# Queries computed in channel rows, the key-token product split at the end of the step, and the vertical box sums done by three accumulating transfers

## The chip, the cores and the metric

The kernel runs on one core of a Trainium2 chip. Its time is the device time of one execution in microseconds (us); lower is better. Before the change it is 1625.53 us, the median of three runs (1621.58 to 1627.81).

## What is computed

Four residual layers are applied in turn to 32 images of 256 channels and 28 x 28 pixels in float32, each on a group-normalised copy of its input:

```python
x = x + _L0_conv_ref(_gn(x), ...)   # gate: sparsemax over 8 experts, then a mixed 1x1 convolution
x = x + _L1_conv_ref(_gn(x), ...)   # 3x3 depthwise, relu, prune, 1x1 convolution, relu, prune
x = x + _L2_conv_ref(_gn(x), ...)   # attention over the 784 pixels ("tokens")
x = x + _L3_conv_ref(_gn(x), 0)     # 3x3 box filter, every weight 1/9
```

The attention squares centred queries and keys and never forms a token-by-token matrix:

```python
q = q - jnp.mean(q, axis=2, keepdims=True); k = k - jnp.mean(k, axis=2, keepdims=True)
q2 = q * q; k2 = k * k
k2n = k2 / (k2s + EPS_DIV); q2n = q2 / (q2s + EPS_DIV)       # sums over the 256 channels
k2n = k2n / jnp.maximum(jnp.linalg.norm(k2n, axis=-2, keepdims=True), EPS_NORM)   # over the tokens
q2n = q2n / jnp.maximum(jnp.linalg.norm(q2n, axis=-1, keepdims=True), EPS_NORM)   # over the channels
kv = jnp.einsum('bnc,bnd->bcd', k2n, v)
out = (v + jnp.einsum('bnc,bcd->bnd', q2n, kv) / math.sqrt(N)) @ Wln + bln
```

## The kernel before

A channel row is a tile of 128 partitions (channels) by 784 columns (pixels); an image has two of them, j = 0 and 1. A token tile has 112 pixels on the partitions and 256 channels in the columns; an image has seven.

**The pipeline.** The program is a hand-written software pipeline. In step t each engine works on seven images at once, called Z, A, B, C_, D, E and F from the youngest to the oldest (Z is image t+1, F is image t-5). Z is loaded and its sums taken; A gets layer 0; B the depthwise convolution; C_ the 1x1 convolution of layer 1; D the queries and keys; E the attention weights and the layer's output; F the box filter and the store. There are 38 steps, t = -1 to 36; from t = 4 to t = 31 the attention stages D and E are both full and A is active too, and these 28 are called full steps below. On each engine the order of the work is the order in which its own `step` function calls the parts, and it never varies; engines wait for each other only through counting semaphores (`wait_ge`).

**TensorE's step**: `value_out(0)`, `key_norms`, `q_to_channels` (two of four pieces), `attention_weights`, `q_to_channels` (two), `value_out(1)`, `gate_logits(A)`, `attention_out` (two), `mix_experts(A)`, `queries_keys(D)`, `pointwise(C_)` and `x2_to_tokens(D)` in turn, `mixed_conv(A)`, `keys_x(D)`, `key_sums(D)`, `group_means`. The last feeds the group norms of all layers, so VectorE's `variances` and `scales_shifts` open the next step.

**Queries before.** `queries_keys` computes queries and keys together, per token tile: a bias matmul and six float32r matmuls of 512 columns. ScalarE squares both halves with running sums (`square_qk`), takes the norms with seven more squares (`q_norms`), and scales the seven tiles (`scale_q`). In the next step TensorE transposes the scaled queries into channel rows (`q_to_channels`, 14 transposes), ScalarE and VectorE copy them as a high and a low part (`q_high`, `q_low`), and `attention_out` reads them. The attention weights come from the product of the keys with the tokens (`keys_x`), which ScalarE and VectorE split into two parts at the start of the next step (`kx_high`, `kx_low`).

**The box filter before.** VectorE adds three columns and then three rows (`box_sums`, four instructions over both halves) and adds a ninth of that to x3 (`make_x4`); SyncE then stores the image.

**PSUM.** `conv_ps` has two banks per half and is used in turn by value and attention output, `pointwise` and `mixed_conv`; `tile_ps` has three banks for everything in tokens and for the attention weights.

Of the kernel before, what the change touches and what calls it, by code (L numbers as in the profile page):

```python
# [5 lines left out]
ALU = mybir.AluOpType  # L6
ACT = mybir.ActivationFunctionType
# [18 lines left out]
BOX_STEPS = 4  # L26
# [15 lines left out]
NORM_EPS = 1e-12  # L42

# [68 lines left out]
def build(nc, x, gate_wT, gate_b, expert_rows, mix_pattern, dw_w, channel_params, pw_wT, w_qk, b_qk, w_vT, w_ln, group_mean, ident, out):  # L112
    with ExitStack() as ctx:  # L113
# [31 lines left out]
        bqk_mean = sb("bqk_mean", [1, 2])  # L145
        b_out = sb("b_out", [P, J])
# [13 lines left out]
        q2 = sb("q2", [TOK, M, C])  # L160
        k2 = sb("k2", [TOK, M, C])
        k4 = sb("k4", [TOK, M, C])
# [4 lines left out]
        qT_parts = sb("qT_parts", [P, 2, J, HW], F32R)  # L167
# [18 lines left out]
        gn_r = sb("gn_r", [P, 4, J])  # L186
        gn_s = sb("gn_s", [P, 4, J])
# [15 lines left out]
        qk_sum = sb("qk_sum", [TOK, 2, M])  # L203
        qk_eps = sb("qk_eps", [TOK, 2, M])
        qk_rec = sb("qk_rec", [TOK, 2, M])
        k_rec2 = sb("k_rec2", [TOK, M])
        q_nsq = sb("q_nsq", [TOK, M])
        q_norm = sb("q_norm", [TOK, M])
        q_alpha = sb("q_alpha", [TOK, 3, M])
# [25 lines left out]
        stored = DmaCount([sem("stored_even"), sem("stored_odd")])  # L235

# [26 lines left out]
        qk_mm = sig("qk_mm", M)  # L263
        q2_ready = sig("q2_ready", M)
        k2_ready = sig("k2_ready", M)
        rec_step = sig("rec_step", 3)
        q4_ready = sig("q4_ready", M)
        q_root = sig("q_root")
        alpha_step = sig("alpha_step", 3)
        qa_ready = sig("qa_ready", M)  # L270
# [14 lines left out]
        qT_mm = sig("qT_mm", 4)  # L285
        qT_hi = sig("qT_hi", 4)
        qT_lo = sig("qT_lo", 4)
# [4 lines left out]
        box_step = sig("box_step", BOX_STEPS)  # L292
        x4_ready = sig("x4_ready", J)
# [11 lines left out]
        def box_operands(n):  # L305


            inner = x3pad[:, :, 1:1 + H, 1:1 + W]
            sums = row_sums[:, :, 1:1 + H, :]
            return [(sums, x3pad[:, :, 1:1 + H, 0:W], inner),  # L310
                    (sums, sums, x3pad[:, :, 1:1 + H, 2:2 + W]),
                    (inner, row_sums[:, :, 0:H, :], sums),
                    (inner, inner, row_sums[:, :, 2:2 + H, :])][n]
# [18 lines left out]

        QUADS = [(j, ms) for j in range(J) for ms in ([0, 1, 2, 3], [4, 5, 6])]

# [25 lines left out]
        def _(sp):  # L360
# [9 lines left out]
            def step(t):  # L370
                Z, F = t + 1, t - 5
# [5 lines left out]
                if F.active:  # L377
                    sp.wait_ge(x4_ready.sem, x4_ready.at(F))
                    sp.dma_start(out_dram[F.times(1)], x3[:, F.odd]).then_inc(stored.of(F), 16)

            run(sp, step)
            for last in (Image(None, IMAGES - 2), Image(None, IMAGES - 1)):
                sp.wait_ge(stored.of(last), stored.at(last))

# [913 lines left out]
```

## Time and profile before

| | |
|---|---|
| Three runs | 1621.58, 1625.53, 1627.81 us |
| Profiled execution, own time | 1624.92 us |
| Its span (first to last instruction) | 1623.1 us, mean granted TensorE clock 0.973 |
| TensorE (PE) busy | 1530.0 us, 94% |
| VectorE (DVE) busy | 1376.0 us, 85% |
| ScalarE (ACT) busy | 1362.3 us, 84% |
| GpSimd (POOL) busy | 189.1 us, 12% |
| DMA | 34 GB/s over the span |

Busy time is the share of the span in which an engine had an instruction under way. Matmuls overlap and their ends are modelled, so what a group of them costs is read from the start of the group to the start of the next one, not from its busy time.

### The profile page before, as it was taken

How to read it: one execution, taken by the hardware profiler on the slowest of the kernel's cores; microseconds unless marked ns; L12 is line 12 of the kernel's file. 1: busy time of each engine (PE TensorE's matmuls, PEld its weight loads, DVE VectorE, ACT ScalarE, POOL GpSimd, SP SyncE). 2: the span in 40 equal slices, each digit the busy share in tenths (PEclk: the TensorE clock that was granted, in tenths of full speed). 3: DMA queues.
4: the chain of work that ended last, by engine and by line, in shares of the span. 5: the costliest groups of instructions: out<-in, count | busy, mean ns of one | idle time of the engine just before them, and what ended most of it. 6: DMA issues, size and time to landing. Idle time of an engine off the chain costs nothing. (4 is left out here: it accounts for less than half of the span.)

```text
span 1623.1 us, 26428 instructions
## 1 busy us (share of the span) xinstructions
PE 1530.0 (94%) x8190; PEld 1149.4 (71%) x8190; DVE 1376.0 (85%) x2466; ACT 1362.3 (84%) x3496; POOL 189.1 (12%) x142
## 2 busy tenths in 40 slices
PE   4469999999999999999999999999999999999993
PEld 2247777777777777777777777777777777776773
DVE  5877689999888998988889998888999988888446
ACT  3368998988999888899998889999888899987862
POOL 1111011011110101111011111101101111010000
PEclk8689999999999999999999999999999999999996
DMA  4000011000111110011111001111100011000001
GB/s 148 20 20 21 21 40 41 31 29 22 40 40 40 40 40 20 20 40 40 40 40 40 20 20 40 40 40 40 40 27 28 24 40 40 21 21 21 21 20 40
DMA packets 21058, 55.58 MB, mean 34 GB/s; under 512 B 2321, under 2 KB 3345, under 8 KB 21010
## 3 DMA queue, kind: packets, MB, share of 16 engines
q1 hardware_dynamic: 20914, 54.98, 9.6%
q8 instruction: 25, 0.41, 0.1%
q14 instruction: 23, 0.19, 0.0%
q10 hardware_dynamic: 96, 0.00, 0.0%
HBM read 29.29 MB, written 25.69 MB: 34 GB/s over the span
## 5 line engine op out<-in xcount | busy, mean ns | idle before, releaser
L770 DVE SCALAR_TENSOR_TENSOR h<-xpad,dw_sb,h 128x784 f32<-128x784 f32 x512 | 495.9, 1031 | 0.0
L541 PE MATMUL tile_ps<-wqk,xn_parts 128*112 128x512 f32 x1344 | 363.8, 425 | 0.0
L541 PEld LDWEIGHTS tile_ps<-wqk,xn_parts 128*112 128x112 f32 x1344 | 235.3, 175 | 79.6
L583 PE MATMUL tile_ps<-k,xT 112*128 112x256 f32 x896 | 205.2, 388 | 7.7 <-ACT xT L1026 7.7
L583 PEld LDWEIGHTS tile_ps<-k,xT 112*128 112x128 f32 x896 | 174.3, 195 | 40.2 <-issue 8.4
L449 PE MATMUL conv_ps<-h,pw_masked 128*128 128x392 f32 x512 | 180.5, 496 | 5.5 <-issue 5.5
L960 ACT ACTIVATE junk<-x 128x784 bf16<-128x784 f32 x192 | 162.3, 848 | 23.6 <-DVE x L797 15.5
L571 PE MATMUL conv_ps<-x,mixed 128*128 128x392 f32 (+1 forms) x512 | 175.1, 494 | 2.2 <-ACT mixed L994 1.1
L1234 POOL TENSOR_SCALAR pw_masked<-pw_sb,hmask 128x256 f32<-128x256 f32 x64 | 119.1, 1869 | 433.9 <-DVE hmask L778 425.5
L1221 POOL TENSOR_SCALAR xpad<-x,gn_r,gn_s 128x784 f32<-128x784 f32 x64 | 64.4, 1013 | 894.2 <-DVE gn_s L701 894.2
L449 PE MATMUL conv_ps<-xn_parts,w_out 128*128 128x392 f32 x768 | 152.7, 347 | 0.0
L449 PE MATMUL conv_ps<-qT_parts,attn_parts 128*128 128x392 f32 x768 | 144.4, 343 | 0.3
L571 PEld LDWEIGHTS conv_ps<-x,mixed 128*128 128x128 f32 x512 | 94.7, 190 | 68.4 <-issue 4.7
L449 PEld LDWEIGHTS conv_ps<-h,pw_masked 128*128 128x128 f32 x512 | 95.5, 192 | 64.6 <-issue 8.6
L1101 ACT ACTIVATE q<-tile_ps 112x256 f32<-112x256 f32 x224 | 86.4, 386 | 62.7 <-PE tile_ps L541 62.6
L449 PEld LDWEIGHTS conv_ps<-qT_parts,attn_parts 128*128 128x128 f32 x768 | 134.9, 188 | 1.5 <-issue 1.5
L449 PEld LDWEIGHTS conv_ps<-xn_parts,w_out 128*128 128x128 f32 x768 | 133.3, 188 | 0.0
L1007 ACT ACTIVATE junk<-x 128x784 bf16<-128x784 f32 x128 | 109.4, 855 | 1.8 <-issue 1.8
L1110 ACT ACTIVATE junk<-q,qk_rec 112x256 bf16<-112x256 f32 x224 | 110.3, 498 | 0.0
L1026 ACT ACTIVATE xT<-tile_ps,qk_rec 112x256 f32<-112x256 f32 x224 | 88.0, 478 | 14.2 <-DVE qk_rec L863 9.8
L1120 ACT ACTIVATE q<-q,q_alpha 112x256 f32<-112x256 f32 x224 | 92.6, 494 | 0.0
L538 PE MATMUL tile_ps<-bqk,ones 128*112 128x512 bf16 x224 | 86.3, 385 | 0.0
(138 smaller groups left out, 2646.9 us busy)
## 6 DMA issues: line engine op xcount, KB each, us to landing
x<-x SPq DMA_DIRECT2D x32, 784.0 KB, 4.3
out<-x SPq DMA_DIRECT2D x32, 784.0 KB, 3.4
expert_sb<-expert_rows SPq DMA_DIRECT2D x8, 256.0 KB, 5.2
x<-w_qk SPq DMA_DIRECT2D x1, 512.0 KB
x<-w_vT SPq DMA_DIRECT2D x1, 256.0 KB
x<-w_ln SPq DMA_DIRECT2D x1, 256.0 KB
pw_sb<-pw_wT SPq DMA_DIRECT2D x1, 256.0 KB
gmean<-group_mean SPq DMA_DIRECT2D x1, 64.0 KB, 3.8
```

Source lines behind the costliest of these rows:

```text
L449: mm = nc.tensor.matmul(conv_ps[:, 2 * j + a, 0:HALF], wt[:, half(j)], act[:, a * HALF:(a + 1) * HALF], start=(first and i == 0), stop=(la ...
L541: mm = nc.tensor.matmul(bank, xn2_parts[:, u, i, m * TOK:(m + 1) * TOK], wqk[:, v, i, :], start=False, stop=(i == J - 1 and u == 1))
L571: mm = nc.tensor.matmul(conv_ps[:, 2 * j + a, 0:HALF + more], mixed[:, i * C + j * P:i * C + (j + 1) * P], x0[:, A.odd, i, a * HALF:(a + 1 ...
L583: mm = nc.tensor.matmul(tile_ps[:, KX_BANK, i * C:(i + 1) * C], xT[:, m, half(i)], k2[:, m, :], start=(m == 0), stop=(m == M - 1))
L770: ins = nc.vector.scalar_tensor_tensor(acc, view, scalar, acc, ALU.mult, ALU.add)
L960: nc.scalar.activation(junk[:, j * HW:(j + 1) * HW], source[:, j, :], ACT.Square, accum_out=gn_in[:, layer, 2 + j:3 + j]).then_inc(gn_sums ...
L1007: nc.scalar.activation(junk[:, j * HW:(j + 1) * HW], x0[:, Z.odd, j, 0:HW], func, accum_out=gn_in[:, 0, first + j:first + j + 1]).then_inc ...
L1026: nc.scalar.activation(xT[:, m, :], tile_ps[0:TOK, XT_BANK[m // 2], m % 2 * C:(m % 2 + 1) * C], ACT.Identity, scale=qk_rec[:, 1, m:m + 1]) ...
L1101: nc.scalar.activation(q2[:, m, :], bank[:, 0:C], ACT.Square, accum_out=qk_sum[:, 0, m:m + 1]).then_inc(q2_ready.sem, 1)
L1110: nc.scalar.activation(junk[0:TOK, m * C:(m + 1) * C], q2[:, m, :], ACT.Square, scale=qk_rec[:, 0, m:m + 1], accum_out=q_nsq[:, m:m + 1]). ...
L1120: nc.scalar.activation(q2[:, m, :], q2[:, m, :], ACT.Identity, scale=q_alpha[:, 2, m:m + 1]).then_inc(qa_ready.sem, 1)
L1234: nc.gpsimd.tensor_scalar(pw_masked[:, j, :], pw_sb[:, j, :], hmask[:, j:j + 1], 0.0, ALU.mult, ALU.add).then_inc(pw_masked_ready.sem, 1)
```

## The change

Queries leave the token tiles. `keys` computes the keys alone (256 columns per token tile); `queries` computes the centred queries directly as channel rows in `conv_ps` (24 matmuls of 392 columns), and ScalarE squares them with the bias (`square_q`) into `q2`, now [128, 2, 784]. The sum over channels that the query norm needs runs over partitions now, so TensorE makes it: ScalarE squares again (`fourth_powers_q`), `query_sums` adds the channels by matmuls against ones (strip s of the partitions holds quarter s of the tokens), ScalarE takes the root, VectorE the reciprocal of a [128, 196] tile, and `query_scales` spreads it over all partitions by four matmuls. VectorE multiplies (`scale_q`), and the high and low parts are made from `q2` in SBUF. `kx_high` and `kx_low` move from the start of step t+1 to the end of step t.

The box filter's scale of 1/9 is folded into the normalisation of x3 (`box_scale`), x3 itself is stored as soon as it is made, VectorE makes only the sums of three columns (`box_row_sums`), and three transfers from GpSimd's queue add the rows above, at and below each row to the stored image in HBM (`add_rows`).

```diff
             def value_out(B, D, E, F, j):
-                wait_free((B, x1_ready, j + 1), (D, y_ready, j + 1), (F, x3_ready, j + 1))
+                wait_free((B, x1_ready, j + 1), (D, y_ready, j + 1), (E, q2_ready, j + 1))
-            def queries_keys(D):
+            def keys(D):
                 pe.wait_ge(xn2_lo.sem, xn2_lo.at(D))
...
-                for m in range(M):
-                    wait_free(*before[m])
-                    bank = tile_ps[0:TOK, QK_BANK[m], :]
-                    nc.tensor.matmul(bank, ones16[:], bqk16[:], start=True, stop=False)
...
+                for b in range(4):
+                    wait_free(*before[b])
+                    for s, m in enumerate(PAIRS[b]):
+                        dst = tile_ps[0:TOK, K_BANK[b], s * C:(s + 1) * C]
+                        nc.tensor.matmul(dst, ones16[:], bqk16[:, C:2 * C], start=True, stop=False)
...
+            def queries(D):
+                for j in range(J):
+                    wait_free((D - 1, x3_ready, j + 1), (D + 2, x1_ready, j + 1))
+                    conv_tile(j, by_parts(wqk[:, :, :, 0:C], xn2_parts)).then_inc(q_mm.sem, 1)
+            def query_sums(D):
+                pe.wait_ge(q4_ready.sem, q4_ready.at(D))
+                pe.wait_ge(xT_ready.sem, xT_ready.at(D, 4))
+                for j in range(J):
+                    for s in range(STRIPS):
+                        mm = nc.tensor.matmul(tile_ps[s * SUB:(s + 1) * SUB, Q4_BANK, 0:QUARTER], ones[:, 0:SUB],
+                                              q4[:, j, s * QUARTER:(s + 1) * QUARTER], start=(j == 0), stop=(j == J - 1),
+                                              skip_group_check=True)
+                mm.then_inc(q4_sum.sem, 1)
+            def query_scales(D):
+                pe.wait_ge(alpha_step.sem, alpha_step.at(D))
+                pe.wait_ge(xT_ready.sem, xT_ready.at(D, 6))
+                for a in range(2):
+                    for s in range(2):
+                        row = (2 * a + s) * SUB
+                        mm = nc.tensor.matmul(tile_ps[:, ALPHA_BANK[a], s * QUARTER:(s + 1) * QUARTER],
+                                              idn[:, row:row + 1].to_broadcast([P, P]), q_alpha[:, 1, :], start=True,
+                                              stop=True)
+                    mm.then_inc(alpha_mm.sem, 1)
...
+            def box_row_sums(F):
+                dve.wait_ge(x3pad_ready.sem, x3pad_ready.at(F))
+                dve.wait_ge(setup_pool, SETUP_POOL)
+                if (F - 1).active:
+                    for rows in rows_added:
+                        dve.wait_ge(rows.of(F - 1), rows.at(F - 1))
+                nc.vector.tensor_tensor(*row_operands(0), ALU.add).then_inc(row_step.sem, 1)
+                dve.wait_ge(row_step.sem, row_step.at(F, 1))
+                nc.vector.tensor_tensor(*row_operands(1), ALU.add).then_inc(row_step.sem, 1)
...
+            def scale_q(D):
+                for a in range(2):
+                    dve.wait_ge(alpha_mm.sem, alpha_mm.at(D, a + 1))
+                    tokens = q2[:, :, a * HALF:(a + 1) * HALF]
+                    nc.vector.tensor_tensor(tokens, tokens, tile_ps[:, ALPHA_BANK[a], 0:HALF].unsqueeze(1).to_broadcast([P, J, HALF]),
+                                            ALU.mult).then_inc(qa_ready.sem, 1)
...
+            def add_rows(F):
+                pool.wait_ge(row_step.sem, row_step.at(F))
+                pool.wait_ge(stored.of(F), stored.at(F))
+                for n in range(BOX_ROWS):
+                    if n:
+                        pool.wait_ge(rows_added[n - 1].of(F), rows_added[n - 1].at(F))
+                    hold(pool, "pool")
+                    rows = row_sums[:, :, n:n + H, :].rearrange("p j h w -> p j (h w)")
+                    pool.dma_start(out_dram[F.times(1)], rows, accum_op=ALU.add).then_inc(rows_added[n].of(F), 16)
```

In the setup TensorE now waits for VectorE's centred bias row before two small matmuls that turn the query bias into a column.

TensorE, a full step, the stretch from the transposes of the queries to the tokens of x2, before (tile names are the program's; `L541` is a matmul of queries and keys, `L466` a transpose; the pair `L538`, `L541` stands seven times, once shown):

```order
L466 MATMUL tile_ps<-idn,q 128x112 x7
L449 MATMUL conv_ps<-xn_parts,w_out 128x392 x12
L440 MATMUL small_ps<-gate_in,ones 128x8 x2
L449 MATMUL conv_ps<-qT_parts,attn_parts 128x392 x24
L558 MATMUL small_ps<-expert_sb,mix_w 32x512 x8
L538 MATMUL tile_ps<-bqk,ones 112x512
L541 MATMUL tile_ps<-wqk,xn_parts 112x512 x6
```

The same stretch after the change, on to the stretch before `mixed_conv` (`L457` with `wqk` is `queries`, `L555` is `query_sums`):

```order
L457 MATMUL conv_ps<-xn_parts,w_out 128x392 x12
L448 MATMUL small_ps<-gate_in,ones 128x8 x2
L457 MATMUL conv_ps<-q_parts,attn_parts 128x392 x24
L585 MATMUL small_ps<-expert_sb,mix_w 32x512 x8
L536 MATMUL tile_ps<-bqk,ones 112x256
L539 MATMUL tile_ps<-wqk,xn_parts 112x256 x6
...
L457 MATMUL conv_ps<-xn_parts,wqk 128x392 x24
L471 MATMUL tile_ps<-idn,xn 112x128 x12
L457 MATMUL conv_ps<-h,pw_masked 128x392 x8
L555 MATMUL tile_ps<-fourth,ones 32x196 x8
L471 MATMUL tile_ps<-idn,xn 112x128 x2
```

The transposes are gone, the seven pairs are half as wide, the queries' 24 matmuls stand behind them, and `query_sums` stands between the 1x1 convolution and the last transposes.

VectorE, a full step, from the box filter to the group norm's sums, before:

```order
L819 TENSOR_TENSOR row_sums<-row_sums,x3pad 128x2x784
L819 TENSOR_TENSOR x3pad<-row_sums 128x2x28x28
L819 TENSOR_TENSOR x3pad<-x3pad,row_sums 128x2x28x28
L770 SCALAR_TENSOR_TENSOR h<-xpad,dw_sb,h 128x784 x7
L859 TENSOR_SCALAR qk_eps<-qk_sum 112x14
...
L870 TENSOR_SCALAR q_alpha<-q_norm 112x7
L872 RECIPROCAL q_alpha<-q_alpha 112x7
L874 SCALAR_TENSOR_TENSOR q_alpha<-q_alpha,qk_rec 112x7
L797 SCALAR_TENSOR_TENSOR x,gn_in<-conv_ps,x 128x784 x2
L770 SCALAR_TENSOR_TENSOR h<-xpad,dw_sb,h 128x784 x5
L687 COPY gn_avg<-small_ps 128x16
```

The same stretch after (`L803` is a tap of the depthwise convolution, `L907` is `scale_q`, `L912` is `kx_low`):

```order
L853 TENSOR_TENSOR row_sums<-row_sums,x3pad 128x2x784
L884 TENSOR_SCALAR k_eps<-k_sum 112x7
...
L803 SCALAR_TENSOR_TENSOR h<-xpad,dw_sb,h 128x784 x9
L895 TENSOR_SCALAR q_alpha<-q_norm 128x196
L900 RECIPROCAL q_alpha<-q_alpha 128x196
L817 TENSOR_SCALAR ymask<-y_over 128x2
L821 SCALAR_TENSOR_TENSOR x,gn_in<-x,ymask 128x784 x2
L830 SCALAR_TENSOR_TENSOR x,gn_in<-conv_ps,x 128x784 x2
L907 TENSOR_TENSOR q<-q,tile_ps 128x2x392 x2
L803 SCALAR_TENSOR_TENSOR h<-xpad,dw_sb,h 128x784 x6
L912 TENSOR_TENSOR kx_parts<-tile_ps,kx_parts 128x512
L713 COPY gn_avg<-small_ps 128x16
```

The key sums' reciprocals now stand ahead of nine taps, the query norm's reciprocal ahead of x2 and x1, and six taps, `scale_q` and `kx_low` stand between x1 and the group norm.

On GpSimd's queue the three accumulating transfers stand behind this step's mask of the 1x1 weights (`mask_weights`) and ahead of the next step's `normalise_x1`, which writes `xpad`; the second and the third each wait for the one before to have landed.

## Rows read from the trace of the kernel before

**Rows 1.** Window of 27 steps: length, busy us of PE, PEld, DVE, ACT, POOL; clock

```profile
138.64:1407.04 1268.40, 1268.31 (x6889) 956.88 (x6889) 1135.86 (x2020) 1142.16 (x2942) 155.09 (x108) 1.00 0.09 33
```

**Rows 2.** TensorE's timeline, one full step: start, length, operation, instructions

```profile
1408.89 0.91 PE L466 MATMUL tile_ps<-idn,q 112*128 112x112 f32 x7
1409.64 0.69 PE L505 MATMUL tile_ps<-bv_ln,k_rows 128*128 128x256 f32 x2
...
1412.02 0.83 PE L466 MATMUL tile_ps<-idn,q 112*128 112x112 f32 x7
1412.62 2.39 PE L449 MATMUL conv_ps<-xn_parts,w_out 128*128 128x392 f32 x12
...
1415.21 4.51 PE L449 MATMUL conv_ps<-qT_parts,attn_parts 128*128 128x392 f32 x24
1419.66 1.92 PE L558 MATMUL small_ps<-expert_sb,mix_w 128*32 128x512 f32 x16
1421.51 0.42 PE L538 MATMUL tile_ps<-bqk,ones 128*112 128x512 bf16 x1
...
1432.79 2.79 PE L449 MATMUL conv_ps<-h,pw_masked 128*128 128x392 f32 x8
1435.42 1.47 PE L474 MATMUL tile_ps<-idn,xn 128*112 128x128 f32 x12
...
1439.58 5.45 PE L571 MATMUL conv_ps<-x,mixed 128*128 128x392 f32 x16
1444.87 6.21 PE L583 MATMUL tile_ps<-k,xT 112*128 112x256 f32 x28
1451.00 0.85 PE L486 MATMUL tile_ps<-k,qk_rec 112*32 112x256 f32 x11
```

**Rows 3.** ScalarE's timeline in a full step, 1x1 convolution's results and a token copy

```profile
829.85 1.04 ACT L1089 ACTIVATE x<-conv_ps,bn_shift,bn_scale 128x784 f32<-128x784 f32 x1
831.00 0.95 ACT L1081 ACTIVATE over<-x,below 128x784 bf16<-128x784 f32 x1
...
831.95 0.46 ACT L1026 ACTIVATE xT<-tile_ps,qk_rec 112x256 f32<-112x256 f32 x1
```

**Rows 4.** VectorE's timeline in the same step, from x1 to the attention weights

```profile
836.66 1.04 DVE L797 SCALAR_TENSOR_TENSOR x<-conv_ps,x 128x784 f32<-128x784 f32 x1
...
838.58 4.82 DVE L770 SCALAR_TENSOR_TENSOR h<-xpad,dw_sb,h 128x784 f32<-128x784 f32 x5
843.32 0.17 DVE L687 COPY gn_avg<-small_ps 128x16 f32<-128x16 f32 x1
...
847.51 1.04 DVE L833 TENSOR_TENSOR qT_parts<-tile_ps,qT_parts 128x448 fp32r<-128x448 f32 x2
848.47 0.62 DVE L767 TENSOR_SCALAR h<-xpad,dw_sb 128x784 f32<-128x784 f32 x1
849.46 0.88 DVE L846 SCALAR_TENSOR_TENSOR attn_parts<-tile_ps,k_inv,attn_parts 128x256 fp32r<-128x256 f32 x2 [0.37 <-ACT attn_parts L1050]
```

**Rows 5.** Groups of instructions by form: count, busy us, mean ns, idle before

```profile
L853 DVE TENSOR_TENSOR xn_parts<-xn,xn_parts 128x784 fp32r<-128x784 f32 x64 | 59.3, 969 | 3.1 <-ACT xn_parts L1058 3.1
L1058 ACT CAST xn_parts<-xn 128x784 fp32r<-128x784 f32 x64 | 51.1, 845 | 11.2 <-PE conv_ps L449 11.2
...
L863 DVE RECIPROCAL qk_rec<-qk_eps 112x14 f32<-112x14 f32 x32 | 7.7, 242 | 1.1
...
L872 DVE RECIPROCAL q_alpha<-q_alpha 112x7 f32<-112x7 f32 x32 | 6.4, 201 | 1.1
```

**Rows 6.** The page's DMA queue and its issues: KB each, us to landing

```profile
q1 hardware_dynamic: 20914, 54.98, 9.6%
...
x<-x SPq DMA_DIRECT2D x32, 784.0 KB, 4.3
out<-x SPq DMA_DIRECT2D x32, 784.0 KB, 3.4
```

**Rows 7.** VectorE's timeline in step 35: first box sum behind the last x3

```profile
1597.65 1.79 DVE L819 TENSOR_TENSOR row_sums<-x3pad 128x1568 f32<-128x1568 f32 x1
```

More of the change, by code:

```diff
@@ L235, in build @@
         stored = DmaCount([sem("stored_even"), sem("stored_odd")])
+        rows_added = [DmaCount([sem(f"rows{n}_added_even"), sem(f"rows{n}_added_odd")]) for n in range(BOX_ROWS)]
         gn = sig("gn", GN_DONE)
@@ L383, in _ @@
                 sp.wait_ge(stored.of(last), stored.at(last))
+                for rows in rows_added:
+                    sp.wait_ge(rows.of(last), rows.at(last))
         @block.tensor
@@ L399, in setup @@
                                               start=(d == 0), stop=(d == J - 1))
+                pe.wait_ge(setup_dve, SETUP_CENTRED)
+                for j in range(J):
+                    nc.tensor.matmul(tile_ps[:, 1, J + j:J + j + 1], bqk_row[:, half(j)], ones[0:1, 0:1], start=True, stop=True)
                 for d in range(J):
@@ L605, in step @@
                 if D.active:
-                    queries_keys(D)
-                if C_.active:
-                    pointwise(C_, range(1))
-                if D.active:
+                    keys(D)
+                    queries(D)
                     x2_to_tokens(D, range(3))
                 if C_.active:
-                    pointwise(C_, range(1, 2))
+                    pointwise(C_, range(2))
                 if D.active:
+                    query_sums(D)
                     x2_to_tokens(D, range(3, 4))
@@ L619, in step @@
                 if D.active:
+                    query_scales(D)
                     keys_x(D)
@@ L886, in step @@
                     scales_shifts(A)
-                if E.active:
-                    kx_low(E)
+                if F.active:
+                    box_scale(A, F)
                 if A.active:
@@ L892, in step @@
                     key_norms(E)
-                    q_low(E, range(2))
+                    q_low(E)
                 if B.active:
@@ L897, in step @@
                     attention_weights_low(E)
-                    q_low(E, range(2, 4))
                 if A.active:
@@ L911, in step @@
                 if F.active:
-                    box_sums(F, range(BOX_STEPS))
-                if B.active:
-                    depthwise(B, slice(3, 10))
+                    box_row_sums(F)
                 if D.active:
@@ L917, in step @@
                 if B.active:
-                    depthwise(B, slice(10, 13))
-                if F.active:
-                    make_x4(F)
+                    depthwise(B, slice(3, 12))
+                if D.active:
+                    q_scales(D)
                 if C_.active:
                     make_x2(C_)
-                if D.active:
-                    q_scales(D)
                 if B.active and not D.active:
-                    depthwise(B, slice(13, None))
+                    depthwise(B, slice(12, None))
                 if A.active:
                     make_x1(A)
+                if D.active:
+                    scale_q(D)
                 if B.active and D.active:
-                    depthwise(B, slice(13, None))
+                    depthwise(B, slice(12, None))
+                if D.active:
+                    kx_low(D)
             run(dve, step)
@@ L1193, in step @@
                 if D.active:
-                    scale_q(D)
+                    q_high(D)
+                    kx_high(D)
             run(act, step)
```

257 lines of the change are left out of this document (122 added, 135 removed).

## Prediction

> **What bounds the kernel now.** I read the table of windows first: over the 27 steps from step 4 to step 31 TensorE is busy for 1268.31 of 1268.40 us at clock 1.00, VectorE for 1135.86 and ScalarE for 1142.16 [rows 1]. A full step takes 1268.40 / 27 = 46.98 us, TensorE has no gap in it, and the other two have some 4.9 and 4.7 us each. So what they are relieved of is worth nothing by itself; what TensorE is given or relieved of counts 28 times, and so does any wait that is put in its way. I then read TensorE's timeline from group start to group start [rows 2], to price its work, and the timelines of ScalarE and VectorE [rows 3, 4], to see when the new links of the chain are done. The last x3 and what comes behind it [rows 7] give the end.
>
> **TensorE's own work, per full step.** Removed: queries and keys together, 1432.79 - 1421.51 = 11.28 us; the transposes of the queries, 1409.64 - 1408.89 = 0.75 and 1412.62 - 1412.02 = 0.60, 1.35 together, their short waits in it [rows 2]. Added:
> - Keys: 49 matmuls of 256 columns. Two rows price a float32r matmul: 24 of 392 columns in 1419.66 - 1415.21 = 4.45 us, 0.185 each, which is 392 / 2.4 = 163 ns and 22 more; 49 of 512 (bias ones among them) in 11.28, 0.230 each, 213 ns and 17 more [rows 2]. With 20 more on 107 ns: 0.128 x 49 = 6.27 us. The lower end is the bare column rate, 5.24.
> - Queries: 24 matmuls of 392 columns as in `attention_out`, 4.45 us.
> - `query_sums`: 8 float32 matmuls, 196 columns, on four strips side by side. `mix_experts` is that with 512 columns: 1421.51 - 1419.66 = 1.85 us [rows 2]. By columns 0.71, half as it stands 0.93; I take 0.9.
> - `query_scales`: 4 float32 matmuls of 196 columns over the whole array. Four of 392 take 1435.42 - 1432.79 = 2.63 us [rows 2], so 1.32; with a change of bank 1.4.
>
> Sum: 6.27 + 4.45 + 0.9 + 1.4 = 13.02 against 12.63: 0.39 us more per step, so TensorE alone would make 47.37. The work moved off the two slower engines is paid by the one that is full.
>
> **The chain through the query norm.** This is new: within the step it starts, TensorE waits for ScalarE and VectorE after the queries. I count from the start of the keys, T = 0. TensorE: keys until 6.27, queries until 10.72, three banks of x2's transposes (1.3) until 12.0, 1x1 convolution until 17.3, `query_sums` 18.2, last transposes 18.4, `mixed_conv` (1444.87 - 1439.58 = 5.29 [rows 2]) 23.7.
> ScalarE is free of the key squares and of x0's sums at about 8.2 (seven squares, four sums, as now), and squares the second half of the queries when they are there, 10.8 to 11.75. Then six token copies at 0.36 (831.95 + 0.36 is where the next group starts): 13.9. Two squares of 784 columns at 0.75, a cast of that size being 0.845 with its overlap [rows 5]: 15.4. Twice (831.00 - 829.85) + (831.95 - 831.00) = 2.10 us for y [rows 3]: 19.6; the last copy and the root of [128, 196]: 20.3.
> VectorE has come there early: two row sums instead of four (two x 1.8 saved, and `make_x4`'s two), but the reciprocal of the key sums is put ahead of the nine taps and waits until 8.2; the taps end near 17.4 and it then idles until 20.3. This idle time is where the relief of VectorE goes. From 20.3:
> - `q_scales`: a reciprocal of 196 columns. Two rows show 201 ns for 7 and 242 ns for 14 [rows 5], 5.9 ns a column, so 242 + 182 x 5.9 = 1.3 us, and 0.33 for the maximum ahead of it: 1.63. The lower bound is one column per cycle as in 784 columns in 969 ns, about 0.36 + 0.33.
> - x2: 2.12 (x1's time and the mask's 0.2); x1: 838.58 - 836.66 = 1.92 [rows 4].
> - `scale_q`: two of 784 columns. The nearest rows are the 969 ns of a subtraction of that size [rows 5]; 1.85 for two.
> - six taps instead of five: 4.74 / 5 x 6 = 5.69 [rows 4].
> - from the group norm to the end of `q_low`'s first pair 848.47 - 843.32 = 5.15, in which `kx_low` already stands [rows 4]; `q_low` is now 1.85 instead of 0.95 (848.47 - 847.51), `box_scale` 0.2: 6.25.
> - one tap 0.55 and the attention weights' low part 0.88 [rows 4].
>
> 1.63 + 2.12 + 1.92 + 1.85 + 5.69 + 6.25 + 0.55 + 0.88 = 20.9, so the weights are ready at 41.2, 0.1 for the signal. Behind them TensorE has `attention_out`, 4.45, and `mix_experts`, 1.85, before the next keys: a step of 47.6 us. TensorE itself would have been there at 47.37 - 6.30 = 41.1, so it waits 0.2 to 0.3. `query_scales` doesn't hold anybody: the scales are there at 22.0, TensorE comes at 23.7, and VectorE takes its result at 26.1. The row transfers need no wait by VectorE in this part either. 47.6 - 46.98 = 0.62, times 28: **+17.4 us**.
> The Trainium skill, VectorE: DVE Perf Modes, in the walkthrough of the 8-slice pipeline, has the reciprocal as an iterative divide with a repeat count of 8. At that, an estimate from its clock of 0.96 GHz, 196 columns take 1.6 us, and the step 0.3 us more, 8 us in all. The two rows show 5.9 ns a column where the page gives 8.3; the rows decide here.
>
> **Edges.** Setup: TensorE waits for the centred bias row, which VectorE makes, ahead of matmuls that it now does earlier; I take 1.5 us, an estimate of mine of less than 0.1%. Steps 3, 32, 33 and 34 have the queries but not all of the rest: 0.6 each, 2.4. In step 35 the transposes' 1.35 and some 0.35 of waits go, and step 34's tail is 0.8 longer: -0.9.
>
> **The end, one accumulating transfer at a time.** Now 1623.1 - 1597.65 = 25.45 us lie behind the last x3 [rows 7]: the box sums and x4 of image 30, the norm, the same for image 31 and a store. After the change image 30's row sums (3.65) are followed by three transfers in series, D each; image 31's row sums must wait for all three, because `row_sums` is one buffer; then its own three. So 3.65 + 3D + 3.65 + 3D, the norm hidden under the first three. The trace shows no accumulating transfer. It reads as much of HBM as a load of x (784 KB, 4.3 us to landing) and writes as much as a store (3.4) [rows 6]. From below D = 3.4, a plain store; from above a whole load and then a whole store, 7.7. The queue's 9.6% of 1623.1 us for 64 such transfers and the weights is some 2.3 us of data each [rows 6]; the read of the destination makes the data twice as much but the landing is waited for once: D = 4.3 + 2.3 = 6.6. That gives 7.3 + 39.6 = 46.9, **+21.4 us**.
> The Trainium skill, DMA: Bandwidth & Descriptors, in the anatomy of one DMA on GpSimd's path, gives 2.0 us and the bytes at 436 GB/s for a plain transfer; an estimate from it is 3.8 us, and the sum would be 17 us less. It says nothing of the read that an accumulation needs.
> Within a full step the transfers are covered: GpSimd's next work is `xpad`, behind the group norm's scales; the norm starts 14.5 us ahead of T (1421.51 [rows 2] - 1407.04, the window's end [rows 1]), so again at 32.5, and with 1.9 for the scales `xpad` is due 34 us after T. The first transfer can start at 6. Two landings and an issue must fit between, so they cost nothing while D is under 13 us. If that cover went, `xpad` would be late, and with it the first tap.
>
> **Sum**, on the profiled execution's 1624.9 us, which is 0.6 below the median: 1624.9 + 17.4 + 1.5 + 2.4 - 0.9 + 21.4 = 1666.7, say **1667 us**, slower by 2.6%.
>
> **Rivals.**
> - R1, TensorE's own work leads (no wait for the attention weights): 0.39 x 28 = 10.9 instead of 17.4, 1660 us. For it: the margin in my chain is only 0.2 us. Chance 0.15.
> - R2, cheap transfers: D near 3.6 with the chain as forecast, 18 less, 1649 us. For it, a store's 3.4; against it, the second stream. 0.15.
> - R3, the transfers hold GpSimd: D over 14.4 us, so that three don't fit in a step of 47.6 less 4 for the sums and their start. At 18 us a step is some 58, 1930 us. Nothing in the rows is near it. 0.05.
> - R4, faster: narrow matmuls issue at the bare column rate. Then the keys are 1.03 us shorter, and as the chain starts behind them, the step is 46.6; with the reciprocal at one column per cycle 46.3 (TensorE's own 46.3): -0.65 x 28 = -18, and with D = 3.4 the end +2. 1611 us. It decides when a 256-column matmul costs under 0.115 us; against it, both measured widths carry 17 to 22 ns. 0.05.
> - R5, no change: a step stays at 47.0 because ScalarE's and VectorE's legs are a little shorter than I count, and the transfers cost a store each: 1624.9 + 3 + 2 = 1630. 0.10.
>
> The forecast itself has 0.50, with a range of its own of 1650 to 1690. A difference of 0.5%, 8 us, is about what a measurement of this kernel can tell from no change. Faster only in R4: 0.05. Within it: R5, 0.10. Slower: 0.85. The range reaches down to 1635 (D = 3.4 with TensorE's own work alone is 1641) and up to 1698 (D = 7.7 and one more us of wait per step is 1701); R3, R4, R5 lie outside.
>
> **What would show it.** Right: full steps of 47.4 to 47.9 us; VectorE idle for 2 to 3 us ahead of the query norm's reciprocal and ahead of the key sums'; TensorE waiting 0.2 to 0.5 us for the attention weights; 256-column matmuls 0.128 us apart; the reciprocal 1.3 us; six transfers in series at the end. Wrong: a step at or under 47.0, a chain whose longest wait is elsewhere (xT, mixed_conv, `row_sums`), or D outside 3.4 to 7.7.

## The result, and the profile after

The changed kernel takes 1646.36 us (median of 4 runs, 1646.04 to 1646.63), the kernel before 1626.18 (4 runs, 1621.58 to 1627.81): a ratio of 1.0129, 95% interval 1.0110 to 1.0147. It is 1.3% slower; the forecast was 1667, its range 1635 to 1698. The profiled execution took 1646.53 us, span 1644.9.

The total is nearer to the forecast than its parts are. The same stretch of 27 full steps as in [rows 1], after; columns as there:

```profile
145.78:1400.31 1254.53, 1254.53 (x7805) 1014.07 (x7804) 1074.74 (x1915) 993.88 (x2050) 250.17 (x186) 1.00 0.39 84
```

A full step is 1254.53 / 27 = 46.46 us instead of 46.98. I had forecast 47.6. TensorE's timeline in one of them, against [rows 2]: the first two rows are one of the seven key tiles, then the last of them, and what follows.

```profile
1366.90 0.32 PE L536 MATMUL tile_ps<-bqk,ones 128*112 128x256 bf16 x1
1366.97 0.96 PE L539 MATMUL tile_ps<-wqk,xn_parts 128*112 128x256 f32 x6
...
1371.88 0.95 PE L539 MATMUL tile_ps<-wqk,xn_parts 128*112 128x256 f32 x6
1372.66 4.46 PE L457 MATMUL conv_ps<-xn_parts,wqk 128*128 128x392 f32 x24
1376.96 1.47 PE L471 MATMUL tile_ps<-idn,xn 128*112 128x128 f32 x12
1378.27 5.43 PE L457 MATMUL conv_ps<-h,pw_masked 128*128 128x392 f32 x16
1383.63 0.87 PE L555 MATMUL tile_ps<-fourth,ones 128*32 128x196 f32 x16
1384.43 0.43 PE L471 MATMUL tile_ps<-idn,xn 128*112 128x128 f32 x2
1384.70 5.45 PE L598 MATMUL conv_ps<-x,mixed 128*128 128x392 f32 x16
1389.98 1.49 PE L567 MATMUL tile_ps<-q_alpha,idn 128*128 128x196 f32 x8
1391.31 6.21 PE L610 MATMUL tile_ps<-k,xT 112*128 112x256 f32 x28
```

From start to start, the keys take 1372.66 - 1366.90 = 5.76 us, the queries 4.30, `query_sums` 0.80, `query_scales` 1.33: 12.19 for the 12.63 that went. VectorE's timeline in a full step, for the chain through the query norm (group starts; the bracket is the idle time ahead of it):

```profile
817.35 0.17 DVE L884 TENSOR_SCALAR k_eps<-k_sum 112x7 f32<-112x7 f32 x1 [1.94 <-ACT k L1133]
...
829.03 0.27 DVE L895 TENSOR_SCALAR q_alpha<-q_norm 128x196 f32<-128x196 f32 x1 [2.56 <-ACT q_norm L1158]
829.33 1.38 DVE L900 RECIPROCAL q_alpha<-q_alpha 128x196 f32<-128x196 f32 x1
...
845.57 2.47 DVE L858 TENSOR_TENSOR q_parts<-q,q_parts 128x784 fp32r<-128x784 f32 x2
847.97 0.61 DVE L800 TENSOR_SCALAR h<-xpad,dw_sb 128x784 f32<-128x784 f32 x1
848.51 0.86 DVE L871 SCALAR_TENSOR_TENSOR attn_parts<-tile_ps,k_inv,attn_parts 128x256 fp32r<-128x256 f32 x2
```

The keys start at 809.36 here. That is T. The query norm is there at T + 19.7 (forecast 20.3), the weights' low part at 849.37, T + 40.0 (forecast 41.2), and TensorE starts `attention_out` at 849.49, 0.1 us later and without a gap that the profile shows. This view can't tell whether TensorE waited there a little or was only just done with its own work; experiments 6 and 7 can.

The end is where the time went. First VectorE behind the last x3, against [rows 7], then GpSimd, then the page's rows on the transfers, against [rows 6]:

```profile
1589.69 1.79 DVE L851 TENSOR_TENSOR row_sums<-x3pad 128x1568 f32<-128x1568 f32 x1
...
1616.37 1.79 DVE L851 TENSOR_TENSOR row_sums<-x3pad 128x1568 f32<-128x1568 f32 x1 [21.70 <-DMA out<-row_sums]
```

```profile
1593.91 1.20 POOL L1270 DMA_DIRECT2D out<-row_sums  x1 [26.15 <-DVE row_sums L853]
1601.60 1.19 POOL L1270 DMA_DIRECT2D out<-row_sums  x1 [6.49 <-DMA out<-row_sums]
1609.23 1.19 POOL L1270 DMA_DIRECT2D out<-row_sums  x1 [6.44 <-DMA out<-row_sums]
1620.60 1.22 POOL L1270 DMA_DIRECT2D out<-row_sums  x1 [10.18 <-DVE row_sums L853]
1628.45 1.21 POOL L1270 DMA_DIRECT2D out<-row_sums  x1 [6.63 <-DMA out<-row_sums]
1635.95 1.20 POOL L1270 DMA_DIRECT2D out<-row_sums  x1 [6.29 <-DMA out<-row_sums]
```

```profile
q0 software_dynamic: 26112, 77.08, 28.8%
...
out<-row_sums POOLq DMA_DIRECT2D x96, 784.0 KB, 7.1
x<-x SPq DMA_DIRECT2D x32, 784.0 KB, 5.5
out<-x SPq DMA_DIRECT2D x32, 784.0 KB, 3.5
```

One accumulating transfer lands after 7.1 us, and the next is issued 7.5 to 7.9 us after the one before. Behind the last x3 there are 1644.9 - 1589.69 = 55.2 us, instead of 25.45.

The whole difference, by stretches of the two profiled executions:

| stretch | before | after | difference | forecast |
|---|---|---|---|---|
| start to the group norm of step 4 | 138.64 | 145.78 | +7.1 | +2.1 |
| 27 full steps | 1268.40 | 1254.53 | -13.9 | +16.7 |
| from there to the last x3 | 190.61 | 189.38 | -1.2 | +1.5 |
| behind the last x3 | 25.45 | 55.2 | +29.8 | +21.4 |
| span | 1623.1 | 1644.9 | +21.8 | +41.8 |

In the first row, step 0 has 28.55 us instead of 24.91, and TensorE's timeline there shows its wait (the second row is the experts' matmuls, on which the mixed weights and then ScalarE's square root for the batch norm wait):

```profile
22.50 1.01 PE L407 MATMUL tile_ps<-ones,xn 1*128 1x1 f32 x4 [4.38 <-DVE xn L684]
...
25.44 2.81 PE L585 MATMUL small_ps<-expert_sb,mix_w 128*32 128x512 f32 x16
```

### The profile page after: what moved, and what is told of

It is laid out like the page before. It is cut to its first block, busy times and chain, and to the rows that moved or that the text cites. A ratio compares the mean times of both kernels' runs of the same rounds, so it can differ in the third digit from the quotient of the medians.

```text
span 1644.9 us, 27605 instructions
## 1 busy us (share of the span) xinstructions
PE 1517.3 (92%) x9282; PEld 1219.7 (74%) x9282; DVE 1296.9 (79%) x2339; ACT 1186.2 (72%) x2440; POOL 304.0 (18%) x238
## 3 DMA queue, kind: packets, MB, share of 16 engines
q0 software_dynamic: 26112, 77.08, 28.8%
## 4 chain that ended last, share of the span: by engine, by line
PE 90%; DVE 4%; DMA 2%; ACT 2%; issue 1%; POOLq 0%; ACTq 0%; DVEq 0%
PE conv_ps L457 35%; PE tile_ps L610 12%; PE tile_ps L539 10%; PE conv_ps L598 9%; PE small_ps L585 4%; PE tile_ps L484 4%; PE tile_ps L471 3%; PE tile_ps L567 3%; PE tile_ps L506 3%; DMA out<-row_sums 2%; PE tile_ps L503 2%; PE tile_ps L536 2%; PE tile_ps L555 2%; DVE h L803 1%; PE small_ps L448 1%
## 5 line engine op out<-in xcount | busy, mean ns | idle before, releaser
L803 DVE SCALAR_TENSOR_TENSOR h<-xpad,dw_sb,h 128x784 f32<-128x784 f32 x512 | 492.5, 1029 | 0.0
L1270 POOL DMA_DIRECT2D out<-row_sums x96 | 115.6, 1204 | 491.9 <-DMA out<-row_sums 411.2
L539 PE MATMUL tile_ps<-wqk,xn_parts 128*112 128x256 f32 x1344 | 187.4, 294 | 0.0
L457 PE MATMUL conv_ps<-h,pw_masked 128*128 128x392 f32 x512 | 176.3, 498 | 5.5 <-issue 5.5
L539 PEld LDWEIGHTS tile_ps<-wqk,xn_parts 128*112 128x112 f32 x1344 | 169.5, 175 | 0.1
L457 PE MATMUL conv_ps<-xn_parts,w_out 128*128 128x392 f32 x768 | 151.0, 345 | 0.0
L1256 POOL TENSOR_SCALAR xpad<-x,gn_rs 128x784 f32<-128x784 f32 x64 | 64.4, 1008 | 455.2 <-DVE gn_rs L727 455.2
L457 PEld LDWEIGHTS conv_ps<-h,pw_masked 128*128 128x128 f32 x512 | 96.1, 193 | 70.6 <-issue 9.4
L457 PE MATMUL conv_ps<-q_parts,attn_parts 128*128 128x392 f32 x768 | 145.3, 345 | 0.0
L457 PE MATMUL conv_ps<-xn_parts,wqk 128*128 128x392 f32 x768 | 142.7, 341 | 0.0
L457 PEld LDWEIGHTS conv_ps<-q_parts,attn_parts 128*128 128x128 f32 x768 | 135.9, 188 | 0.4 <-DVE attn_parts L871 0.3
L457 PEld LDWEIGHTS conv_ps<-xn_parts,wqk 128*128 128x128 f32 x768 | 135.7, 188 | 0.0
L457 PEld LDWEIGHTS conv_ps<-xn_parts,w_out 128*128 128x128 f32 x768 | 134.5, 188 | 0.0
L1142 ACT ACTIVATE q<-conv_ps,bq_col 128x784 f32<-128x784 f32 x64 | 58.6, 915 | 50.4 <-PE conv_ps L457 50.2
L1133 ACT ACTIVATE k<-tile_ps 112x256 f32<-112x256 f32 x224 | 84.2, 381 | 8.0 <-PE tile_ps L539 7.9
```

The lines of the kernel that those rows point to most:

```text
L457: mm = nc.tensor.matmul(conv_ps[:, 2 * j + a, 0:HALF], wt[:, half(j)], act[:, a * HALF:(a + 1) * HALF], start=(first and i == 0), stop=(la ...
L539: mm = nc.tensor.matmul(dst, xn2_parts[:, u, i, m * TOK:(m + 1) * TOK], wqk[:, v, i, C:2 * C], start=False, stop=(i == J - 1 and u == 1))
L803: ins = nc.vector.scalar_tensor_tensor(acc, view, scalar, acc, ALU.mult, ALU.add)
L1133: nc.scalar.activation(k2[:, m, :], tile_ps[0:TOK, K_BANK[m // 2], m % 2 * C:(m % 2 + 1) * C], ACT.Square, accum_out=k_sum[:, m:m + 1]).th ...
L1270: pool.dma_start(out_dram[F.times(1)], rows, accum_op=ALU.add).then_inc(rows_added[n].of(F), 16)
```

## The experiments

All ratios are against runs of the kernel before on the same chip. A step's time is that between two starts of VectorE's copy of the group means, over the same 27 full steps; the windows shown are those.

**1. The queries alone.** The changed kernel, with the box sums, x4 and the store as before:

```
-                    pool.dma_start(out_dram[F.times(1)], rows, accum_op=ALU.add)
+                nc.vector.tensor_tensor(*row_operands(2), ALU.add).then_inc(row_step.sem, 1)
+                nc.vector.tensor_tensor(*row_operands(3), ALU.add).then_inc(row_step.sem, 1)
...
+                    nc.vector.tensor_tensor(x4, x3pad[:, j, 1:1 + H, 1:1 + W], x4, ALU.add)
```

> The query part of the change without the box part: VectorE makes all four box sums and x4 again, and the store stands behind x4. Theory 1 (the two halves of the change need each other): VectorE gets two more sums of 128x1568 (1.8 us each) ahead of the key sums' reciprocal and two adds for x4 (0.97 us each) behind the query scales. The first 3.65 us are partly taken by its idle 1.94 and 2.56 us of the changed kernel; the 1.94 us of x4 lie in the chain from the query norm to the attention weights, which has no slack. So full steps of about 48.3 us instead of 46.46 (+53 us over 28), the end back to some 25 us behind the last x3 (-30): 1670 us. Theory 2 (TensorE's own work leads and VectorE has room): steps stay at 46.46, only the end goes back: 1617 us.

Measured: 1671.83 us, ratio 1.0281 (1.0266 to 1.0297). The window of 27 steps, and TensorE ahead of `attention_out` in one step:

```profile
146.25:1453.39 1307.14, 1271.21 (x7817) 1025.94 (x7815) 1212.53 (x2019) 993.08 (x2050) 153.73 (x108) 0.99 0.09 32
```

```profile
1121.29 4.55 PE L457 MATMUL conv_ps<-q_parts,attn_parts 128*128 128x392 f32 x24 [1.46 <-DVE attn_parts L878]
```

A step is 48.41 us, TensorE is idle for 35.9 us of the window, and the wait named is the one expected, that for the attention weights' low part. Theory 1 holds. Made alone, the query part of the change costs 2.8%.

**2. The transfers alone.** The kernel before with row sums, early store and three accumulating transfers; queries and keys untouched:

```
-                    box_sums(F, range(BOX_STEPS))
+                    box_row_sums(F)
-                if F.active:
-                    make_x4(F)
...
+                if F.active:
+                    add_rows(F)
```

> The box part of the change on the kernel of before: row sums on VectorE, three accumulating transfers, the store ahead; queries and keys as they were. Theory 1: full steps stay at 46.98 us, since TensorE has no gap and its work is the same, and the transfers are hidden in them; the end grows from 25.45 us to 7.3 + 6 x 7.7 = 53.5, so +28: about 1654 us. Theory 2: less work on VectorE and ScalarE makes full steps shorter too, as in the changed kernel (46.5 us, -14): 1640 us. Theory 3: the transfers disturb x's loads or GpSimd in the steps, which then are over 47.2 us: above 1660.

Measured: 1645.27 us, ratio 1.0121 (1.0105 to 1.0136).

```profile
139.35:1400.21 1260.86, 1260.86 (x6886) 956.08 (x6886) 1008.89 (x1942) 1136.50 (x2942) 252.43 (x186) 1.00 0.41 84
```

The end is as in theory 1: from the group norm of step 34 on it has 28.1 us more than before. But a step is 46.70, not 46.98, with the same matmuls: between the two theories. So the kernel before had 0.28 us of waiting in each step that its window, "busy for 1268.31 of 1268.40", doesn't show. TensorE's timeline has the place of most of it: the second row starts 0.74 us after the first, and the third 0.26 after the second.

```profile
1355.86 0.91 PE L469 MATMUL tile_ps<-idn,q 112*128 112x112 f32 x7
1356.60 0.61 PE L508 MATMUL tile_ps<-bv_ln,k_rows 128*128 128x256 f32 x2
1356.86 1.06 PE L511 MATMUL tile_ps<-w_out,kx_parts 128*128 128x256 f32 x6
```

Before, in the step at 1360, the same two distances are 0.86 and 0.35, 0.21 us more, and VectorE's low part of the key-token sums, for which these matmuls wait, ends just as they start:

```profile
1361.99 0.91 PE L466 MATMUL tile_ps<-idn,q 112*128 112x112 f32 x7
1362.85 0.70 PE L505 MATMUL tile_ps<-bv_ln,k_rows 128*128 128x256 f32 x2
1363.20 1.06 PE L508 MATMUL tile_ps<-w_out,kx_parts 128*128 128x256 f32 x6
```

One view of the kernel before does name this wait: not in TensorE's matmuls but in its weight loads. From 420 to 1360 us the list of waits has `PEld tile_ps L505 <- DVE kx_parts L879: 3.6, 20, 0.2`, which is 3.6 us in 20 steps; the same list of this experiment has no such line. The lists of the other two engines point to a loop through both of them as what leads. VectorE waits 1.6 us a step for ScalarE's query norm, and ScalarE 0.5 us a step for VectorE's reciprocal of the sums (`ACT xT L1026 <- DVE qk_rec L863: 9.4, 19, 0.6`), ahead of which the four box sums stand. With two of them gone the second wait is gone too.

**3. The last two images on VectorE.** The changed kernel, with the 30 other images' vertical sums by transfers:

```
+        def by_vector(F):
+            return F.pair is None and F.offset >= VECTOR_FROM      # VECTOR_FROM = IMAGES - 2
...
                     box_row_sums(F)
+                    if by_vector(F):
+                        box_columns(F)
...
-                if F.active:
+                if F.active and not by_vector(F):
                     add_rows(F)
```

> The changed kernel, but the last two images have their vertical sums and x4 on VectorE and a plain store; the 30 others use the transfers. Theory 1 (the end is the six transfers in series and nothing else): behind the last x3 at 1590 us there are again some 25 to 27 us, so a span of about 1616 and 1618 us, 0.5% faster than before. Theory 2 (what the end costs is something else, such as the drain of earlier transfers, which the store waits for): above 1630 us.

Measured: 1617.56 us, ratio 0.9948 (0.9934 to 0.9961). The last x3 is done at 1591.00 us, the span ends at 1617.0: 26.0 us. Theory 1 holds. Against the changed kernel 28.8 us are saved, more than the 20 us that the change loses: that is what the six transfers in series cost beyond the same work on VectorE.

**4. The bias matmuls later.** The changed kernel, with the two matmuls on the centred bias row behind the experts':

```
                     mix_experts(A)
+                if t.first:
+                    setup_bias()
```

> The changed kernel with the two matmuls on the centred bias row behind the experts' matmuls in step 0, so that TensorE doesn't wait 4.38 us for VectorE ahead of them. Theory 1 (step 0's extra 3.64 us come from that wait through the mixed weights and ScalarE's square root for the batch norm): step 0 back to about 25 us, in all 1642.8 us. Theory 2 (VectorE's own setup sets step 0): 1646 us as it was.

Measured: 1642.88 us, ratio 1.0100 (1.0085 to 1.0116). Step 0 has 25.10 us, and the order in TensorE's timeline is

```profile
19.18 1.92 PE L588 MATMUL small_ps<-expert_sb,mix_w 128*32 128x512 f32 x16
22.44 0.60 PE L413 MATMUL tile_ps<-ones,xn 1*128 1x1 f32 x4 [1.33 <-DVE xn L689]
```

Theory 1 holds. The prediction had 1.5 us for this wait; it was 3.5.

**5. Halved columns.** The kernel before, its 512-column matmuls as pairs of 256:

```
-                    nc.tensor.matmul(bank, ones16[:], bqk16[:], start=True, stop=False)
+                    for cols in (slice(0, C), slice(C, 2 * C)):
+                        nc.tensor.matmul(bank[:, cols], ones16[:], bqk16[:, cols], start=True, stop=False)
```

> The kernel of before, with every 512-column matmul of queries and keys as two of 256 columns, 98 instead of 49 per full step, and nothing else. It prices the narrow matmul in the old surroundings. Theory 1 (a narrow matmul carries about the same 17 to 22 ns as a wide one, as the prediction had it): 98 x 0.128 = 12.54 us instead of 11.28, a full step 1.26 us longer, 29 of them: about 1662 us. Theory 2 (what the changed kernel showed, 0.1176 us each, is the price of the width): 98 x 0.1176 = 11.52, +0.24 us a step, about 1633 us. Theory 3 (the changed kernel's pitch has to do with its surroundings): somewhere between.

Measured: 1627.07 us, ratio 1.0006 (0.9997 to 1.0016). The first and the last of the 14 groups, and what follows:

```profile
1375.01 0.32 PE L539 MATMUL tile_ps<-bqk,ones 128*112 128x256 bf16 x1
...
1385.66 0.96 PE L542 MATMUL tile_ps<-wqk,xn_parts 128*112 128x256 f32 x6
1386.45 1.81 PE L449 MATMUL conv_ps<-h,pw_masked 128*128 128x392 f32 x5
```

11.44 us for 98, 0.1167 each: the width's own price, in old surroundings too, and theory 1 is out. The time is 1.6 us above the kernel before, not the 7 of theory 2, for the 0.16 us that TensorE does more per step don't appear: 27 steps take 1268.67 us instead of 1268.40. They went into the wait of experiment 2, whose two distances are now some 0.84 and 0.35 us in one step and 0.75 and 0.28 in the next. In the kernel before, the loop through VectorE and ScalarE led by some 0.2 us, not TensorE.

**6. A second reciprocal.** The changed kernel, with the chain 1.3 us longer:

```
                 nc.vector.reciprocal(q_alpha[:, 1, :], q_alpha[:, 0, :]).then_inc(alpha_step.sem, 1)
+                nc.vector.reciprocal(q_again[:], q_alpha[:, 0, :])
```

> The changed kernel with the reciprocal of 196 columns of the query norm made twice on VectorE, the second time into a tile that nobody reads. It adds 1.3 to 1.4 us to VectorE behind the query norm. Theory 1 (TensorE's own work and the chain through the query norm end within 0.1 us of each other, so the chain has no slack): full steps of 46.46 + 1.2 = 47.7 us, in all about 1681 us. Theory 2 (TensorE leads with a margin of over a microsecond): 1646 us as it was.

Measured: 1684.15 us, ratio 1.0359 (1.0343 to 1.0375). 27 steps take 1290.07 us, 47.78 each, 1.32 more, the length of the reciprocal; TensorE waits ahead of `attention_out`:

```profile
1016.33 4.55 PE L458 MATMUL conv_ps<-q_parts,attn_parts 128*128 128x392 f32 x24 [1.12 <-DVE attn_parts L872]
```

So the chain has no slack.

**7. No reciprocal.** The opposite, a chain 1.1 us shorter; this kernel leaves out the division by the query norm:

```
-                nc.vector.reciprocal(q_alpha[:, 1, :], q_alpha[:, 0, :])
+                nc.vector.tensor_scalar(q_alpha[:, 1, :], q_alpha[:, 0, :], 1.0, None, ALU.mult)
```

> The changed kernel with the reciprocal of the query norm replaced by a multiplication by 1 (the division by the norm is left out), so that VectorE's chain is some 1.1 us shorter per step. Theory 1 (TensorE's own work leads, the chain is just behind): full steps stay at 46.46, 1646 us. Theory 2 (the chain leads and TensorE waits for it in small pieces): full steps shorter by up to a few tenths, 1638 to 1643 us.

Measured: 1640.95 us, ratio 1.0090 (1.0075 to 1.0106). By the total this looks like theory 2. By the steps it is theory 1:

```profile
145.23:1399.47 1254.24, 1254.24 (x7804) 1013.17 (x7804) 1049.47 (x1915) 989.67 (x2051) 250.19 (x186) 1.00 0.40 84
```

1254.24 / 27 = 46.45, as it was. Nearly all of the gain lies at the end, where less work covers the chain: steps 32 to 34 have 42.98, 41.29 and 41.11 us instead of 44.93, 42.43 and 43.19. In the changed kernel TensorE's own work leads in a full step, and the chain is right behind it (experiment 6).

**8. Transfers that don't accumulate**, and **9. transfers of half the channels**, both on the changed kernel; 8 leaves out the vertical sums and the residual, 9 the vertical sums of each image's second 128 channels:

```
-                    pool.dma_start(out_dram[F.times(1)], rows, accum_op=ALU.add)
+                    pool.dma_start(out_dram[F.times(1)], rows)                                      # 8
+                    pool.dma_start(out_dram[F.times(1)][:, 0], rows[:, 0], accum_op=ALU.add)        # 9
```

> The changed kernel with the three transfers of row sums not accumulating: the same bytes from the same tile by the same queue, each overwriting the image (the vertical sums and the residual are so left out). Theory 1 (the read of the destination is what an accumulating transfer costs beyond a store): from issue to issue some 4.8 us instead of 7.7, so 6 x 2.9 = 17 us less at the end, 1629 us, full steps unchanged. Theory 2 (the cost is that of GpSimd's queue and of the way there and back): 7.7 us as before, 1646 us.

> The changed kernel with the accumulating transfers carrying the first 128 channels only, 392 KB instead of 784 KB (the vertical sums of the other channels are left out). Known: 7.1 us to landing for the full accumulating transfer, 3.8 for the full plain one. Theory 1 (one fixed time, the rest by bytes): with 2.0 us fixed, 4.6 to landing, 5.1 from issue to issue, 15 us less at the end, 1631 us. Theory 2 (the way there and back is made twice, the read ahead of the write, so two fixed times): 5.6 to landing, 6.2 from issue to issue, 9 us less, 1637 us. Theory 3 (bytes don't matter): 1646 us.

Measured: 1627.62 us for 8, ratio 1.0013 (1.0004 to 1.0022), and 1635.05 for 9, ratio 1.0053 (1.0038 to 1.0068). Of the page of 8, and then of 9:

```profile
q0 software_dynamic: 13824, 77.08, 11.9%
...
out<-row_sums POOLq DMA_DIRECT2D x96, 784.0 KB, 3.8
```

```profile
out<-row_sums POOLq DMA_DIRECT2D x96, 392.0 KB, 4.8
```

A plain transfer of the same bytes lands after 3.8 us. The Trainium skill, DMA: Bandwidth & Descriptors, in the anatomy of one DMA on GpSimd's path, has 2.0 us and the bytes at 436 GB/s; an estimate from it is 3.8 us, and for a plain transfer the trace agrees. The accumulating one takes 7.1 us, with nearly twice the packets (26112 for 13824), and doesn't follow that formula. Between 392 and 784 KB it grows from 4.8 to 7.1: 2.3 us for 392 KB, so 4.6 us that go with the bytes and 2.5 that don't. That is nearer to theory 1 of run 9 (4.6) than to theory 2 (5.6), and so is the time from issue to issue at the end, 5.3 to 5.4 us for theory 1's 5.1 and theory 2's 6.2. The total is not: 1635.05 us lies nearer to theory 2's 1637 than to 1631. Some 2 us of that lie in the last wait of SyncE's queue, for TensorE's (3.9 us for 1.7 in the changed kernel), which neither theory had; why it is longer is open. So what the accumulation adds goes mostly with the bytes, as far as two sizes can show. The full steps of both stay at 46.46 us.

**10. The key-token sums split early, alone.** The kernel before, with the third part of the change only:

```
-                if E.active:
-                    kx_low(E)
                 if A.active:
                     gate_logits(A)
...
                     depthwise(B, slice(13, None))
+                if D.active:
+                    kx_low(D)
```

ScalarE's `kx_high` moved likewise.

> The kernel of before with one thing of the change alone: the two parts of the key-token sums are made at the end of the step in which the sums arise, on ScalarE and VectorE, and not at the start of the next, behind the group norm. Theory 1 (in the kernel before, TensorE waits some 0.2 to 0.3 us per full step for these parts, unseen inside the time of its matmuls, and the changed kernel owes half of its gain per step to that): full steps of 46.7 instead of 46.98 us, about 8 us less, 1618 us. Theory 2 (the wait is one for VectorE as a whole, and only the relief by the box sums takes it away): 1626 us as before.

Measured: 1639.83 us, ratio 1.0080 (1.0067 to 1.0094). Slower, which neither theory had. A step is 1280.73 / 27 = 47.43 us. VectorE now waits at the end of the step for ScalarE's part, ahead of the group norm:

```profile
852.87 0.69 DVE L879 TENSOR_TENSOR kx_parts<-tile_ps,kx_parts 128x512 fp32r<-128x512 f32 x1 [1.15 <-ACT kx_parts L1127]
```

ScalarE's part stands there behind its scaling of the seven query tiles. TensorE's wait for the key-token sums is gone from the list of waits, but VectorE's new one costs more, and TensorE now waits 0.5 us a step for ScalarE's copy `k_rows` and 0.3 for its `k_norm`, for which it didn't before. So theory 1's gain isn't there, and what the place of the split would be worth without these new waits, this run can't tell. That the relief by the box sums takes the 0.28 us away without the split, experiment 2 shows. Which of the operations taken from VectorE would be enough was not tried; the list of waits there points at the two ahead of the reciprocal of the sums.

**11. Both edges mended**: 3 and 4 together, a version that beats both kernels.

> The changed kernel with both edges mended: the last two images' vertical sums and x4 on VectorE with a plain store, and the two bias matmuls of the setup behind the experts' matmuls. If the two gains are independent they add: 1646.4 - 28.8 - 3.5 = 1614 us, 0.7% faster than before. If step 0's gain is taken back by a later wait: 1617.5 us.

Measured: 1614.11 us (5 runs, 1612.24 to 1615.09), ratio 0.9930 (0.9916 to 0.9943). The gains add up: 1646.4 - 28.8 - 3.5 = 1614.1.

## Why the prediction was right or wrong

- **Direction and range: right, the direction in part by luck.** The time lies 21 us below the forecast, in the range of 1635 to 1698 but outside the 1650 to 1690 of the forecast's own case. That case (the chain leads, 47.6 us a step) is not what happened: the full steps were to lose 16.7 us and gained 13.9, and only the ends made the kernel slower. By mechanism the rival R1 is nearest, since TensorE's own work leads, though with less of it than R1 had. By the number R2 (1649) is nearer, but its cheap transfers are not what was found.
- **"Keys: 49 matmuls ... 0.128 x 49 = 6.27 us": the step that failed.** They took 5.76, 0.1176 each. I had added a fixed 20 ns to the column time, as from the two widths shown. Measured: 256 columns 0.1167 to 0.1176 us, 392 columns 4.30 / 24 = 0.179, 512 columns 0.230. That is 0.46, 0.46 and 0.45 ns a column; what I read as a fixed cost goes mostly with the width. (The 24 of `attention_out` take 4.45 us before and 4.47 after, 0.186 each; why those of `queries` take less is open.) With it the queries (4.30 for 4.45), `query_sums` (0.80 for 0.9) and `query_scales` (1.33 for 1.4; no run shows the 0.08 us that I had added for a change of bank) were too dear, together by 0.83 us. R4 was built on this very price, with 0.115 us as the point where it decides; the runs came close to that, and I had given it 0.05.
- **"TensorE has no gap in it": a misreading, 0.28 us.** The base of the sum, 46.98, held a wait that hid inside the groups' times; experiments 2 and 5 show it. Steps then went 46.98, less 0.28 by the relief of experiment 2 (46.70), less 0.24 by TensorE's work (46.46). Of the latter the four terms give 0.44; some 0.2 us come back where groups of matmuls follow each other in a new order (the 1x1 convolution with x2's transposes takes 6.94 us without `query_sums`, for 6.80 in experiment 2). The full step was off by 47.6 - 46.46 = 1.14 us: 0.83 and 0.28, less these 0.20, and the 0.23 of waiting for the weights that didn't come.
- **The chain: right in mechanism, late by 1.2 us.** Weights at T + 40.0 for 41.2: 0.66 because keys and queries are shorter, and most of the rest because VectorE waits 0.27 us for the group norm's root instead of 0.78; that `q_low` takes 0.6 more is made up for by two other small terms (no wait ahead of `kx_low`, shorter gate products). Both idle times of VectorE, 1.94 and 2.56 us, are where they were forecast. That the chain has no slack is shown by experiment 6, and that a shorter chain gains nothing in a full step, by 7: TensorE leads, by next to nothing.
- **The reciprocal: right**, 1.30 us from start to start for 1.3. An estimate from the repeat count of 8 in the Trainium skill, VectorE: DVE Perf Modes, in the walkthrough of the 8-slice pipeline, was 1.6 us; the trace doesn't agree, at 6.6 to 7 ns a column. `q_low` was too cheap, 2.47 us for 1.85. GpSimd writes `xpad` at that time; whether that is the cause was not tried.
- **"D = 4.3 + 2.3 = 6.6": right in mechanism, the term too small.** It is 7.1 us to landing and 7.7 from issue to issue, which is the upper bound of 7.7. Six times 1.1 is most of the 8.4 us that the end was off. That the transfers are hidden in a full step is right: the steps of experiments 8 and 9, with shorter transfers, are the same.
- **Setup: 1.5 for 3.5 us.** I priced the wait and not what hangs on it: the experts' matmuls, then the mixed weights, then ScalarE's root, then VectorE. The other edges: step 3 is 1.6 us longer, forecast 0.6. Step 2's 1.8 may in part be the clock's and not the change's: the same 16 matmuls of the 1x1 convolution took 8.56 us in the profile of experiment 4 and 7.21 in that of experiment 11, with the same code up to there, at a granted clock of 0.64 and 0.76; in the changed kernel 7.88, at 0.70, and before 7.04, at 0.78.

So the expected loss came, for another reason: the steady part of the kernel gained 14 us, and the two ends, which the change touches by the way, lost 36, up to 2 of which may be the clock's.

## What to carry to other kernels

Before a "full" engine's time is taken as its work, look whether its groups of equal instructions take equally long from step to step: a wait of 0.1 us doesn't show as idle time of its matmuls. The list of waits of its weight loads can show it. A change that trades work for latency (a transfer for an addition) is priced at the drain, where nothing covers it; there the old way can be kept for the last images alone, at little code. And two halves of a change may need each other: here +2.8% and +1.2% alone make +1.3% together, because the one frees the engine that the other fills.

## What the runs showed of the hardware that I had not expected

- By two sizes, an accumulating transfer takes 2.5 us and another 2.3 for each 392 KB (4.8 and 7.1 us to landing); a plain one of 784 KB takes 3.8 us. The issue of an accumulating one of 784 KB takes GpSimd 1.20 us, that of a plain one 0.74. In the kernel with accumulating transfers of 784 KB loads of x take 5.5 us to landing, before and with plain ones 4.3.
- Splitting a float32r matmul of 512 columns into two of 256 costs 0.003 us (0.2334 for 0.230).
